# Turning sorted token rows by a transposing DMA instead of on TensorE, in a fused attention and mixture-of-experts kernel

## The chip, the cores and the metric

The kernel runs on one core of a Trainium2 chip. The metric is the device time of one execution in microseconds, from the first to the last work of the core; smaller is better. Each engine of the core (TensorE = PE, VectorE = DVE, ScalarE = ACT, GpSimd = POOL, SyncE = SP) has its own instruction stream, and they meet at semaphores. SP does no arithmetic here: it issues DMAs.

## The reference

Input are 8 x 1024 tokens of 128 channels, in float32. The layer is

```
xn  = layernorm(x)
out = x + attention(xn) + ffn(xn)

attention: off = xn @ W_off, w = softmax(xn @ W_attn) over 4 points of 8 heads
           s[token] = sum over 32 of  xn[batch, first token, idx(off)] * w
           result = broadcast(s) @ W_out + b_out

ffn(x, w1, w2, w3) = silu(x @ w1.T) * (x @ w3.T) @ w2.T       (128 -> 256 -> 128)
ffn part:  two shared experts for every token,
           + top 2 of 8 routed experts, weighted by a softmax over the 2 logits
```

## The kernel before, in words

Matmuls with float32 accuracy are made of fp16 ones: every token row x is kept as a high half and a low half (fp16 each), every weight too, and a first-layer product is three matmuls, high x high, high x low, low x high. The second layer multiplies float32 tiles.

The work goes in three stages. First (to about 85 us of the profile) x is loaded, normalised, split, turned and projected. Then (to about 257 us) the two shared experts run for 16 blocks of 512 tokens, and beside them the routing, the attention's gather (one-hot matrices that 32 transposing DMAs of line 459 turn) and the sorting: GpSimd scatters all 8192 token rows to the DRAM tensor `sorted_rows`, so that tokens with the same pair of experts stand together. A row of it has 137 words: 64 words with the 128 high halves, 64 with the 128 low halves, 8 expert weights, and the token's place in the output (`CW` = 128, `DEST` = 136).

The last stage, the one that is changed, runs the routed experts. The sorted rows are 64 tiles of 128 rows. A main job is one tile with the two experts of its first row: 24 first-layer matmuls, 8 second-layer matmuls. Where another pair begins inside a tile, 27 extra experts are done in 14 extra jobs, which load their tiles a second time. The list is `JOBS`, 78 jobs: main tiles 0 to 7, the 14 extra jobs, main tiles 8 to 63.

The first layer wants the tokens with the channels on the partitions, so each tile must be turned. Two main tiles make a step (32 steps). "Turn" n is the n-th entry of `TURN_ORDER` (46 entries: 4 main steps, 14 extras, 28 main steps). For each turn, before:

- SP loads it in the loop of lines 481 to 495: `rows<-sorted_rows` (line 485) for a main step, up to two `proj<-sorted_rows` (line 478) for an extra job. It runs up to `AHEAD` = 8 turns ahead, and waits for `d_turn`, the count of turns done on PE (line 483). The same loop issues the 16 writes of the attention's part of the output, `out_dram<-base` (line 471, `write_block`), at turns listed in `WRITE_AT`; the last two come right after the load of turn 26.
- PE turns it (`r_turn`, line 700: four transposes of 128 x 128 against the identity, to PSUM), counts `d_turn`.
- ACT copies the result from PSUM to a ring of four slots `xrT` in `units` (`r_xt`, line 886), counts `d_xt`.
- PE reads the ring in the first layer (`r_first`, lines 724 to 726).

PE's stream is software pipelined: iteration s does turn of job s, then the second layer of job s-4 (`r_second`, line 751), then the first layer of job s-2. After each job ACT applies silu (line 900), DVE multiplies (`r_hf`, line 1342, the tile `hbuf`) and, after the second layer, adds the result with its weight to `yt` in two steps (`y_first`, `y_second`, lines 1386 and 1404, for extras 1393 and 1409). Iterations 0 to 21 of DVE also add the attention's part (line 1415). The expert weights come from the same loaded rows (`side_products`, line 1354). The matrix `sides`, which these need, is made once by two PE matmuls (`spread_sides`, line 684), as part of turn 0, and an ACT copy (line 889).

GpSimd sends each finished tile to the output by an accumulating scatter (`r_send`, line 951). It starts when all 16 blocks of line 471 have landed (`out_done`) and the last extra job (job 21) is added, and then follows `d_y`, one scatter a main tile.

Of the kernel before, what the change touches and what calls it, by code (L numbers as in the profile page):

```python
# [44 lines left out]
NE = E + NSH  # L45
# [3 lines left out]
RING = 4  # L49
# [13 lines left out]
CW, DEST = 128, 136  # L63
UNROLL = 8
# [149 lines left out]
def layer_kernel(nc, x, wall, wproj, bproj, w_out, b_out, const, out, sorted_rows, y_rows):  # L214
    with ExitStack() as ctx:
# [87 lines left out]
        xr = rows[:].rearrange("p (r k) w -> p r k w", k=2)  # L303
        xrT = units[:, 4:6, :].bitcast(F16).rearrange("p i c -> p (i c)").rearrange("p (r k s c) -> p r k s c", r=RING, k=2, s=2)
# [14 lines left out]
        xr16 = xr.bitcast(F16)  # L319
        xr32 = xr.bitcast(F32)  # L320
# [93 lines left out]
        sorted_steps = sorted_rows.rearrange("(s k p) w -> s p k w", k=2, p=P)  # L414
        sorted_tiles = sorted_rows.rearrange("(t p) w -> t p w", p=P)
        out_rows = out.rearrange("b s c -> (b s) c")

        def rows_landed(eng, step):

            n = TURN_ORDER.index(step)  # L420
            before = sum(1 if s < MAIN_STEPS else min(2, EXTRAS - 2 * (s - MAIN_STEPS)) for s in TURN_ORDER[n % AHEAD:n + 1:AHEAD])
            eng.wait_ge(d_in[n % AHEAD], 16 * before)

        def rows16_of(job, k):

            return xr16[:, job.step, k] if job.main else xe16[:, 2 * job.i + k]
# [5 lines left out]
        def _(sp):  # L432
# [48 lines left out]
            for n, step in enumerate(TURN_ORDER):  # L481
                if n >= AHEAD:
                    sp.wait_ge(d_turn, n + 1 - AHEAD)
                if step < MAIN_STEPS:
                    sp.dma_start(xr[:, step], sorted_steps[step]).then_inc(d_in[n % AHEAD], 16)
                else:
                    if step == MAIN_STEPS:
                        sp.wait_ge(hot_ready, BATCH)
                        sp.wait_ge(aw_ready, 2 * BATCH)
                        sp.wait_ge(extras_ready, 1)  # L490
                    for a in range(2 * (step - MAIN_STEPS) + 1, min(2 * (step - MAIN_STEPS) + 2, EXTRAS) + 1):
                        load_extra(a, d_in[n % AHEAD])
                for i in range(NB):
                    if n == WRITE_AT[i]:
                        write_block(i)
# [6 lines left out]
        def _(pe):  # L502
# [185 lines left out]
            def r_turn(g, r):  # L688

                job = JOBS[UNROLL * g + r]  # L690
                if not job.turns:
                    return
                rows_landed(pe, job.step)
                if job.turn == 0:
                    pe.wait_ge(w_split, NE)
                if job.turn >= 2:
                    pe.wait_ge(d_xt, job.turn - 1)
                for k in range(2 if job.main else job.experts):
                    for s in range(2):
                        mm = pe.transpose(pT16[:, job.turn % 2, k, s, :], rows16_of(job, k)[:, s * P:(s + 1) * P], c["ident"][:])  # L700
                mm.then_inc(d_turn, 1)
                if job.turn == 0:
                    spread_sides()

            def r_first(g, r):
# [3 lines left out]
                pe.wait_ge(d_xt, job.turn + 1)  # L709
# [53 lines left out]
        def _(act):  # L763
# [110 lines left out]

            def r_xt(g, r):

                job = JOBS[UNROLL * g + r]
                if not job.turns:
                    return
                act.wait_ge(d_turn, job.turn + 1)  # L880
                if job.turn == 0:
                    act.wait_ge(v_done, APAIRS)
                if job.turn >= RING:
                    act.wait_ge(d_l1, LAST_OF_TURN[job.turn - RING] + 1)
                n = 2 if job.main else job.experts
                nc.scalar.copy(xrT[:, job.turn % RING, 0:n], pT16[:, job.turn % 2, 0:n]).then_inc(d_xt, 1)  # L886
                if job.turn == 0:
                    act.wait_ge(sides_done, 1)
                    nc.scalar.copy(sides.rearrange("p t k e -> p (t k e)"), pY[:].rearrange("p b c -> p (b c)")).then_inc(sides_ready, 1)
# [17 lines left out]
        def _(pool):  # L907
# [36 lines left out]
            def r_send(job):  # L944

                t = job.t
                pool.wait_ge(d_y, max(job.place, LAST_EXTRA) + 1)
                if t >= OUT_SEMS:
                    pool.wait_ge(d_out[t % OUT_SEMS], 16 * (t // OUT_SEMS))
                pool.sem_inc(pool_go, 1)  # L950
                pool.indirect_dma_start(out_rows, bass.IndirectOffsetOnAxis(ap=xr[:, job.step, t % 2, DEST:DEST + 1].bitcast(U32), axis=0),  # L951
                                        yt[:, t], None, bounds_check=TOK - 1, oob_is_err=False,
                                        compute_op=ALU.add).then_inc(d_out[t % OUT_SEMS], 16)
# [10 lines left out]
        def _(dve):  # L964
# [380 lines left out]
            def side_products(g, r):  # L1345

                job = JOBS[UNROLL * g + r]
                if job.main and job.turns:
# [5 lines left out]
                    v.tensor_tensor(side_scr[:, job.step % 2], xr32[:, job.step, :, CW:CW + E].unsqueeze(2).broadcast_to([P, 2, 2, E]),  # L1354
# [108 lines left out]
```

## Time and profile before

| | |
|---|---|
| median of 3 runs | 462.47 us (460.53 to 462.51) |
| the profiled execution's own time | 464.75 us |
| its span in the profile | 462.9 us |
| PE busy, of the span | 392.8 us (85%) |
| DVE busy | 344.3 us (74%) |
| ACT busy | 173.4 us (37%) |
| POOL busy | 198.5 us (43%) |
| mean clock granted to PE | 0.946 of full |

The profile is of one execution. Busy shares are means over three stages with different limits, so the last stage (from about 258 us to the end) must be read by itself. Matmul durations overlap (each is shown from its start to its modelled end), so what one costs is the distance between starts, which the chain of waits shows.

### The profile page before, as it was taken

The numbers are of one execution on the slowest core, as the hardware profiler recorded it, in microseconds if no ns is written. First come the engines' busy times: TensorE is split into PE (matmuls) and PEld (weight loads), VectorE is DVE, ScalarE is ACT, GpSimd is POOL, SyncE is SP. The second block draws the span as 40 slices with busy tenths as digits, with TensorE's granted clock in tenths as the row PEclk, the third lists the DMA queues.
The fourth block names the chain that finished last, engine by engine and source line by source line (L and its number), as shares of the span: only waits on it lengthen the run. The fifth ranks groups of instructions, "written<-read, shape, count | busy, mean of one in ns | idle before, by whom it ended". The sixth has DMA issues, their size and how long they took to land.

```text
span 462.9 us, 12949 instructions
## 1 busy us (share of the span) xinstructions
PE 392.8 (85%) x4485; PEld 331.9 (72%) x4485; DVE 344.3 (74%) x1093; ACT 173.4 (37%) x321; POOL 198.5 (43%) x169
## 2 busy tenths in 40 slices
PE   0555876797899999998959899999999999999990
PEld 0445733464566776666638699999999999999990
DVE  5976898989847689999999878875554555555561
ACT  3797754147212222221202334443333334333330
POOL 0432402054856544344360000002888876666664
PEclk9965897899999999999988999999999999999995
DMA  8700000010245557777626154443555554432332
GB/s 298 187 2 1 1 1 1 0 33 23 65 145 96 101 120 146 145 144 130 128 30 140 44 151 151 126 130 79 72 62 62 63 69 56 66 31 26 31 31 23
DMA packets 68791, 37.14 MB, mean 80 GB/s; under 512 B 39425, under 2 KB 62337, under 8 KB 68737
## 3 DMA queue, kind: packets, MB, share of 16 engines
q1 hardware_dynamic: 57040, 27.62, 25.3%
q0 software_dynamic: 11264, 8.69, 14.1%
q8 instruction: 34, 0.56, 0.5%
q14 instruction: 21, 0.16, 0.1%
q10 hardware_dynamic: 432, 0.11, 0.1%
HBM read 15.13 MB, written 12.88 MB: 61 GB/s over the span
## 4 chain that ended last, share of the span: by engine, by line
PE 52%; DVE 31%; issue 6%; ACT 6%; POOL 1%; DMA 1%; DVEq 1%; POOLq 0%; ACTq 0%
PE pY L751 16%; PE pAB L724 8%; PE pAB L726 8%; PE pAB L725 7%; DVE hbuf L1073 5%; ACT units L789 4%; DVE small L1257 4%; DVE aw L1241 3%; PE pY L591 3%; DVE hot L1228 3%; PE pAB L576 2%; PE pAB L578 2%; PE pAB L577 2%; PE pV L700 2%; DVE attn_all L1267 2%
## 5 line engine op out<-in xcount | busy, mean ns | idle before, releaser
L951 POOL DMA_INDIRECT out_dram<-xT,rows x64 | 99.0, 1547 | 105.6 <-DVE xT L1393 68.2
L724 PE MATMUL pAB<-units,wsp 128*128 128x128 f16 x620 | 108.4, 219 | 0.6 <-issue 0.2
L726 PE MATMUL pAB<-units,wsp 128*128 128x128 f16 x620 | 108.4, 219 | 0.0
L725 PE MATMUL pAB<-units,wsp 128*128 128x128 f16 x620 | 108.4, 219 | 0.0
L936 POOL DMA_INDIRECT sorted_rows<-rows,slot x64 | 70.0, 1094 | 82.4 <-DVE hbuf L1073 55.5
L1342 DVE SCALAR_TENSOR_TENSOR hbuf<-pAB,units 128x512 f32<-128x512 f32 x78 | 53.7, 688 | 67.8 <-PE pAB L726 52.2
L853 ACT ACTIVATE units<-pAB 128x512 f32<-128x512 f32 x64 | 38.0, 596 | 137.0 <-PE pAB L578 113.7
L751 PE MATMUL pY<-wsp,hbuf 128*128 (+1 forms) x620 | 86.9, 282 | 1.4 <-DVE xT L1404 0.7
L900 ACT ACTIVATE units<-pAB 128x512 f32<-128x512 f32 x78 | 46.4, 594 | 102.8 <-PE pAB L726 102.8
L751 PEld LDWEIGHTS pY<-wsp,hbuf 128*128 128x128 f32 x620 | 75.6, 192 | 2.3 <-issue 0.9
L576 PE MATMUL pAB<-xT,wsp 128*128 (+1 forms) x128 | 50.5, 394 | 26.4 <-DVE hbuf L1073 26.1
L591 PE MATMUL pY<-wsp,hbuf 128*128 128x128 f32 x512 | 71.5, 284 | 0.0
L591 PEld LDWEIGHTS pY<-wsp,hbuf 128*128 128x128 f32 x512 | 67.0, 196 | 4.7 <-issue 0.3
L1073 DVE SCALAR_TENSOR_TENSOR hbuf<-pAB,units 128x512 f32<-128x512 f32 x64 | 49.9, 781 | 16.7 <-ACT units L853 8.2
L724 PEld LDWEIGHTS pAB<-units,wsp 128*128 (+1 forms) x620 | 60.8, 98 | 2.0 <-issue 1.5
L725 PEld LDWEIGHTS pAB<-units,wsp 128*128 (+1 forms) x620 | 60.7, 98 | 0.9
L726 PEld LDWEIGHTS pAB<-units,wsp 128*128 (+1 forms) x620 | 60.6, 98 | 0.1
L577 PE MATMUL pAB<-xT,wsp 128*128 (+1 forms) x128 | 50.2, 392 | 0.0
L578 PE MATMUL pAB<-xT,wsp 128*128 (+1 forms) x128 | 50.0, 391 | 0.0
L576 PEld LDWEIGHTS pAB<-xT,wsp 128*128 128x128 f16 x128 | 12.8, 100 | 39.7 <-DVE hbuf L1073 22.0
L886 ACT COPY units<-pV 128x512 f16<-128x512 f16 (+1 forms) x46 | 26.7, 581 | 19.5 <-PE pV L700 19.4
L914 POOL TENSOR_TENSOR rows<-units,rows 128x512 f32 (+1 forms) x16 | 17.9, 1120 | 35.3 <-DVE rows L1050 35.3
(150 smaller groups left out, 538.3 us busy)
## 6 DMA issues: line engine op xcount, KB each, us to landing
rows<-sorted_rows SPq DMA_DIRECT2D x32, 137.0 KB
base<-in_x SPq DMA_DIRECT2D x8, 512.0 KB, 7.5
out_dram<-base SPq DMA_DIRECT2D x16, 256.0 KB, 2.5
wraw<-in_wall SPq DMA_DIRECT2D x10, 256.0 KB
proj<-sorted_rows SPq DMA_DIRECT2D x27, 68.5 KB
wsp<-in_wall SPq DMA_DIRECT2D x10, 128.0 KB
sorted_rows<-rows,slot POOLq DMA_INDIRECT x64
out_dram<-xT,rows POOLq DMA_INDIRECT x64
```

What stands on the lines that cost most here:

```text
L576: pe.matmul(bank[:, u % 2, :], whi[:, x, w], xi(0), start=True, stop=False)
L577: pe.matmul(bank[:, u % 2, :], whi[:, x, w], xi(1), start=False, stop=False)
L578: mm = pe.matmul(bank[:, u % 2, :], wlo[:, x, w], xi(0), start=False, stop=True)
L591: mm = pe.matmul(o, hbuf[:, u % 4, t], second[:, h, x, :], start=False, stop=(u % 4 == 3), skip_group_check=True)
L724: pe.matmul(o, hi, x(0), start=True, stop=False)
L725: pe.matmul(o, hi, x(1), start=False, stop=False)
L726: mm = pe.matmul(o, lo, x(0), start=False, stop=True)
L751: mm = pe.matmul(o, hbuf[:, q % 4, c0:c0 + P], w, start=(h == 0), stop=(h == 1))
L936: pool.indirect_dma_start(sorted_rows, bass.IndirectOffsetOnAxis(ap=slot[:, t:t + 1].bitcast(U32), axis=0), rows[:, t, :], None, bounds_ch ...
L951: pool.indirect_dma_start(out_rows, bass.IndirectOffsetOnAxis(ap=xr[:, job.step, t % 2, DEST:DEST + 1].bitcast(U32), axis=0), yt[:, t], No ...
L1073: v.scalar_tensor_tensor(hbuf[:, u % 4, :], pB[:, u % 2, :], 1 / (XS * WS), silu[:, u % 2, :], ALU.mult, ALU.mult).then_inc(hf_done, 1)
L1342: v.scalar_tensor_tensor(hbuf[:, q % 4, 0:job.cols], pAB[:, 2 * (q % 2) + 1, 0:job.cols], 1 / (XS * WS), silu[:, q % 2, 0:job.cols], ALU.m ...
```

## The change

For main steps the transposing is taken off PE and ACT. SP now issues two DMAs a step: one of the 9 last words of each row (`meta`, weights and destination), and one transposing DMA that reads the 256 fp16 halves of 256 rows and writes them turned to a place of their own for every step (`xrT` is now the first 64 x 128 words of `rows`, `meta` the last 64 x 9). There is no ring for them, and `r_first` waits for the landing itself. Extra jobs stay as they were, with the ring renamed `xeT`. SP's look-ahead now waits for `d_l1`, the first layer of the last job of the turn eight before, in place of `d_turn`. `spread_sides` stands at the head of the first layer of job 0, and the copy of `sides` ahead of ACT's loop.

```diff
-        xr = rows[:].rearrange("p (r k) w -> p r k w", k=2)
-        xrT = units[:, 4:6, :].bitcast(F16).rearrange("p i c -> p (i c)").rearrange("p (r k s c) -> p r k s c", r=RING, k=2, s=2)
+        row_words = rows[:].rearrange("p t w -> p (t w)")
+        xr_flat = row_words[:, 0:TILES * CW].bitcast(F16)
+        xrT = xr_flat.rearrange("p (r s k c) -> p r s k c", r=MAIN_STEPS, s=2, k=2)
+        meta = row_words[:, TILES * CW:TILES * ROWW].rearrange("p (t m) -> p t m", m=META)
+        xeT = units[:, 4:6, :].bitcast(F16).rearrange("p i c -> p (i c)").rearrange("p (r k s c) -> p r k s c", r=RING, k=2, s=2)
...
+        sorted_halves = sorted_rows.bitcast(F16).rearrange("(s q) w -> s q w", q=2 * P)
...
             for n, step in enumerate(TURN_ORDER):
                 if n >= AHEAD:
-                    sp.wait_ge(d_turn, n + 1 - AHEAD)
+                    sp.wait_ge(d_l1, LAST_OF_TURN[n - AHEAD] + 1)
                 if step < MAIN_STEPS:
-                    sp.dma_start(xr[:, step], sorted_steps[step]).then_inc(d_in[n % AHEAD], 16)
+                    sp.dma_start(meta[:, 2 * step:2 * step + 2], sorted_steps[step][:, :, CW:ROWW]).then_inc(d_in[n % AHEAD], 16)
+                    sp.dma_start(xrT[:, step].rearrange("p s k c -> p s (k c)"), sorted_halves[step][:, 0:2 * P],
+                                 transpose=True).then_inc(d_in[n % AHEAD], 16)
...
             def r_turn(g, r):
 
                 job = JOBS[UNROLL * g + r]
-                if not job.turns:
+                if job.main:
                     return
                 rows_landed(pe, job.step)
-                if job.turn == 0:
-                    pe.wait_ge(w_split, NE)
-                if job.turn >= 2:
-                    pe.wait_ge(d_xt, job.turn - 1)
-                for k in range(2 if job.main else job.experts):
+                if job.i >= 2:
+                    pe.wait_ge(d_xt, job.i - 1)
+                for k in range(job.experts):
...
                 mm.then_inc(d_turn, 1)
-                if job.turn == 0:
-                    spread_sides()
 
             def r_first(g, r):
...
-                pe.wait_ge(d_xt, job.turn + 1)
+                if q == 0:
+                    pe.wait_ge(w_split, NE)
+                    spread_sides()
+                if not job.main:
+                    pe.wait_ge(d_xt, job.i + 1)
+                elif job.turns:
+                    rows_landed(pe, job.step)
...
-                        x = lambda s: xrT[:, job.turn % RING, job.t % 2 if job.main else k, s, :]
+                        x = lambda s: xrT[:, job.step, s, job.t % 2, :] if job.main else xeT[:, job.i % RING, k, s, :]
...
+            act.wait_ge(sides_done, 1)
+            nc.scalar.copy(sides.rearrange("p t k e -> p (t k e)"), pY[:].rearrange("p b c -> p (b c)")).then_inc(sides_ready, 1)
+
             def r_xt(g, r):
 
                 job = JOBS[UNROLL * g + r]
-                if not job.turns:
+                if job.main:
                     return
...
-                n = 2 if job.main else job.experts
-                nc.scalar.copy(xrT[:, job.turn % RING, 0:n], pT16[:, job.turn % 2, 0:n]).then_inc(d_xt, 1)
-                if job.turn == 0:
-                    act.wait_ge(sides_done, 1)
-                    nc.scalar.copy(sides.rearrange("p t k e -> p (t k e)"), pY[:].rearrange("p b c -> p (b c)")).then_inc(sides_ready, 1)
+                nc.scalar.copy(xeT[:, job.i % RING, 0:job.experts], pT16[:, job.i % 2, 0:job.experts]).then_inc(d_xt, 1)
```

Two places show how the instruction streams move. On PE, late in the last stage, where the turn of a main step stood ahead of a second layer (names are output <- inputs; the rows named ISA are register work, which sets the address of the next expert's weights). Before:

```order
L726 MATMUL pAB<-units,wsp 128x128
L672 ISA
L700 MATMUL pV<-c_ident,rows 128x128 [waits d_xt,d_in4]
L700 MATMUL pV<-c_ident,rows 128x128 x3
L751 MATMUL pY<-wsp,hbuf 128x128 [waits d_y,d_hf]
L677 ISA
```

and with the change:

```order
L730 MATMUL pAB<-rows,wsp 128x128
L674 ISA
L755 MATMUL pY<-wsp,hbuf 128x128 [waits d_y,d_hf]
L679 ISA
L755 MATMUL pY<-wsp,hbuf 128x128
L679 ISA
```

The four transposes of a main step are gone, and the landing of the rows (`d_in4`) is now waited for by the first matmul of the first layer. On SP, at the two last writes of line 471, before:

```order
L485 DMA rows<-sorted_rows 128x2x137 [waits d_turn]
L471 DMA out_dram<-base 128x512 [waits attn_added]
L485 DMA rows<-sorted_rows 128x2x137 [waits d_turn] x2
L471 DMA out_dram<-base 128x512 [waits attn_added] x2
L485 DMA rows<-sorted_rows 128x2x137 [waits d_turn] x19
```

and with the change:

```order
L485 DMA rows<-sorted_rows 128x2x9 [waits d_l1]
L486 DMA_TRANSPOSE rows<-sorted_rows 128x2x256
L471 DMA out_dram<-base 128x512 [waits attn_added]
L485 DMA rows<-sorted_rows 128x2x9 [waits d_l1]
L486 DMA_TRANSPOSE rows<-sorted_rows 128x2x256
L485 DMA rows<-sorted_rows 128x2x9 [waits d_l1]
L486 DMA_TRANSPOSE rows<-sorted_rows 128x2x256
L471 DMA out_dram<-base 128x512 [waits attn_added] x2
```

Each load is two DMAs, and the two last writes now stand behind a wait for `d_l1` instead of `d_turn`.

## Rows read from the trace of the kernel before

**Rows 1.** The page, part 1: busy time, share of the span, instructions.

```profile
PE 392.8 (85%) x4485; PEld 331.9 (72%) x4485; DVE 344.3 (74%) x1093; ACT 173.4 (37%) x321; POOL 198.5 (43%) x169
```

**Rows 2.** Windows of the last stage: length, engines' busy time, granted clock, DMA share, GB/s.

```profile
260.00:275.00 15.00, 14.44 (x183) 12.60 (x182) 11.39 (x39) 5.79 (x10) 0.00 (x0) 1.00 0.44 112
275.00:315.00 40.00, 40.00 (x572) 39.72 (x570) 32.46 (x119) 18.46 (x33) 0.00 (x0) 1.00 0.47 145
315.00:360.00 45.00, 44.31 (x624) 43.83 (x624) 25.27 (x76) 16.41 (x28) 32.54 (x21) 1.00 0.47 60
360.00:400.00 40.00, 40.00 (x570) 39.81 (x568) 22.39 (x66) 14.83 (x25) 28.53 (x19) 1.00 0.51 65
400.00:450.00 50.00, 50.00 (x708) 49.59 (x707) 28.30 (x84) 17.74 (x30) 31.74 (x21) 1.00 0.34 32
```

**Rows 3.** The chain of waits, 366 to 385 us: start, length, what.

```profile
370.67 0.95 PE pY L751 x8
372.95 0.22 PE pV L700 x4
373.18 0.95 PE pY L751 x8
375.46 0.95 PE pY L751 x8
...
377.75 0.22 PE pV L700 x4
```

**Rows 4.** PE in order of time, 256 to 260 us: start, length, instructions, idle before.

```profile
258.46 0.38 PE L700 MATMUL pV<-c_ident,rows 128*128 128x128 f16 x4 [0.56 <-issue]
259.54 0.59 PE L684 MATMUL pY<-hot,c_ones 128*128 128x512 f16 x2 [0.69 <-DVE base L1083]
259.97 0.39 PE L700 MATMUL pV<-c_ident,rows 128*128 128x128 f16 x4
```

**Rows 5.** Groups by line, whole program: busy us, mean ns, idle before.

```profile
L700 PE MATMUL pV<-c_ident,rows 128*128 128x128 f16 x128 | 12.4, 219 | 0.6 <-issue 0.6
L886 ACT COPY units<-pV 128x512 f16<-128x512 f16 (+1 forms) x46 | 26.7, 581 | 19.5 <-PE pV L700 19.4
```

**Rows 6.** SP's DMAs: line 459 (issue ns min/median/max; landing), then line 485's first four.

```profile
L459 SPq DMA_TRANSPOSE units<-hot x32: 1232/1350/1904, 144.9 to 247.6; - x32
...
DMA to landing us min/median/max: 3.2/3.8/5.8
...
248.99 2.15 SPq L485 DMA_DIRECT2D rows<-sorted_rows  x4
```

**Rows 7.** Windows with four transposing DMAs (145 to 155), with four row loads (249 to 252).

```profile
145.00:150.00 5.00, 5.00 (x33) 3.41 (x31) 5.00 (x24) 1.19 (x2) 3.31 (x4) 1.00 0.88 143
150.00:155.00 5.00, 5.00 (x34) 3.63 (x32) 4.09 (x15) 1.32 (x3) 2.51 (x3) 1.00 1.03 156
...
249.00:252.00 3.00, 3.00 (x33) 2.16 (x32) 2.96 (x12) 0.60 (x1) 0.00 (x0) 1.00 0.95 209
```

**Rows 8.** SP's last two writes (line 471), their landing, and DVE after job 23.

```profile
311.20 0.94 SPq L471 DMA_DIRECT2D out_dram<-base  x2
...
DMA to landing us min/median/max: 2.1/2.5/4.5
...
319.20 0.69 DVE L1342 SCALAR_TENSOR_TENSOR hbuf<-pAB,units 128x512 f32<-128x512 f32 x1 [0.40 <-PE pAB L726]
```

**Rows 9.** POOL in order of time: scatters 1, 29, 30 and 64 of line 951.

```profile
321.12 1.58 POOL L951 DMA_INDIRECT out_dram<-xT,rows  x1 [68.25 <-DVE xT L1393]
...
373.05 1.55 POOL L951 DMA_INDIRECT out_dram<-xT,rows  x1 [0.30 <-issue]
375.55 1.54 POOL L951 DMA_INDIRECT out_dram<-xT,rows  x1 [0.95 <-DVE xT L1404]
...
455.97 1.54 POOL L951 DMA_INDIRECT out_dram<-xT,rows  x1 [0.31 <-DMA out_dram<-xT,rows]
```

**Rows 10.** POOL's sorting scatters, 140 to 235 us, beside the transposing DMAs: ns min/median/max.

```profile
L936 POOL DMA_INDIRECT sorted_rows<-rows,slot x41: 966/971/1407, 140.0 to 231.8; - x41
```

More of the change, by code:

```diff
@@ L63 @@
 CW, DEST = 128, 136
+META = ROWW - CW
 UNROLL = 8
@@ L318, in layer_kernel @@
         rows32 = rows[:].bitcast(F32)
-        xr16 = xr.bitcast(F16)
-        xr32 = xr.bitcast(F32)
+        meta32 = meta.bitcast(F32)
         xe16 = xe.bitcast(F16)
@@ L420, in rows_landed @@
             n = TURN_ORDER.index(step)
-            before = sum(1 if s < MAIN_STEPS else min(2, EXTRAS - 2 * (s - MAIN_STEPS)) for s in TURN_ORDER[n % AHEAD:n + 1:AHEAD])
+            before = sum(2 if s < MAIN_STEPS else min(2, EXTRAS - 2 * (s - MAIN_STEPS)) for s in TURN_ORDER[n % AHEAD:n + 1:AHEAD])
             eng.wait_ge(d_in[n % AHEAD], 16 * before)
-        def rows16_of(job, k):
-            return xr16[:, job.step, k] if job.main else xe16[:, 2 * job.i + k]
         block = ctx.enter_context(nc.Block())
@@ L869, in _ @@
             straight(UNITS, UNITS + 3, both)
+            act.wait_ge(sides_done, 1)
+            nc.scalar.copy(sides.rearrange("p t k e -> p (t k e)"), pY[:].rearrange("p b c -> p (b c)")).then_inc(sides_ready, 1)
             def r_xt(g, r):
                 job = JOBS[UNROLL * g + r]
-                if not job.turns:
+                if job.main:
                     return
-                act.wait_ge(d_turn, job.turn + 1)
-                if job.turn == 0:
+                act.wait_ge(d_turn, job.i + 1)
+                if job.i == 0:
                     act.wait_ge(v_done, APAIRS)
-                if job.turn >= RING:
-                    act.wait_ge(d_l1, LAST_OF_TURN[job.turn - RING] + 1)
-                n = 2 if job.main else job.experts
-                nc.scalar.copy(xrT[:, job.turn % RING, 0:n], pT16[:, job.turn % 2, 0:n]).then_inc(d_xt, 1)
-                if job.turn == 0:
-                    act.wait_ge(sides_done, 1)
-                    nc.scalar.copy(sides.rearrange("p t k e -> p (t k e)"), pY[:].rearrange("p b c -> p (b c)")).then_inc(sides_ready, 1)
+                if job.i >= RING:
+                    act.wait_ge(d_l1, [j.place for j in JOBS if j.i == job.i - RING][0] + 1)
+                nc.scalar.copy(xeT[:, job.i % RING, 0:job.experts], pT16[:, job.i % 2, 0:job.experts]).then_inc(d_xt, 1)
             def r_silu(g, r):
@@ L950, in r_send @@
                 pool.sem_inc(pool_go, 1)
-                pool.indirect_dma_start(out_rows, bass.IndirectOffsetOnAxis(ap=xr[:, job.step, t % 2, DEST:DEST + 1].bitcast(U32), axis=0),
+                pool.indirect_dma_start(out_rows, bass.IndirectOffsetOnAxis(ap=meta[:, t, DEST - CW:DEST - CW + 1].bitcast(U32), axis=0),
                                         yt[:, t], None, bounds_check=TOK - 1, oob_is_err=False,
@@ L1353, in side_products @@
                         dve.wait_ge(share_ready, job.step - 1)
-                    v.tensor_tensor(side_scr[:, job.step % 2], xr32[:, job.step, :, CW:CW + E].unsqueeze(2).broadcast_to([P, 2, 2, E]),
+                    v.tensor_tensor(side_scr[:, job.step % 2], meta32[:, 2 * job.step:2 * job.step + 2, 0:E].unsqueeze(2).broadcast_to([P, 2, 2, E]),
                                     sides[:, 2 * job.step:2 * job.step + 2], ALU.mult).then_inc(side_parts, 1)
```

2 lines of the change are left out of this document (1 added, 1 removed).

## The prediction

> **What bounds the kernel now.** I read the page first, then the windows of the last stage, then the chain of waits there. The page gives PE as the busiest engine [rows 1], but 85% over the whole span does not say where it is the limit. The windows do: from 275 us to 450 us PE is busy in 40.00 of 40.00, 44.31 of 45.00, 40.00 of 40.00 and 50.00 of 50.00 us, at the full granted clock (1.00, 2.4 GHz), while DVE has 32.46 of 40.00 at first and then some 56% [rows 2]. The reader should see two things: no engine but PE is full, and the clock column leaves no room for a gain or a loss by the clock. The chain then shows what PE's time is made of. From one second layer to the next PE needs 2.29 us a job (373.18 to 375.46), and in front of every other job stand four transposes of line 700, 0.22 us long (372.95); two jobs take 377.75 - 372.95 = 4.80 us [rows 3]. Nothing but PE stands in that piece of the chain. So in this stage a microsecond off PE is a microsecond off the end, until another engine or a load is late.
>
> **What is removed.** The 32 main steps have 4 transposes each, 128 in all [rows 5]. The busy column there (12.4 us) overstates them, since matmuls overlap; the distance in the chain, 0.22 us for four, is what they cost [rows 3]. One of the 32 turns is free today: turn 0 runs at 258.46, while PE would wait anyway for DVE's line 1083 (the idle 0.69 before line 684 at 259.54) [rows 4]. Turn 1, at 259.97, stands between `spread_sides` and the first first layer and counts [rows 4]. That leaves 31 x 0.22 = 6.8 us. ACT loses 32 copies of 0.58 us, 18.6 us [rows 5], but it is busy for some 37% there [rows 2], so I cost this at nothing. The cover is PE: the copy is never in the chain.
>
> **What is added on SP and the DMA engines.** No transposing DMA from DRAM is in the trace; the nearest rows are the 32 that turn `hot` inside SBUF, of 256 KB each, twice the bytes of a step. Their issue takes 1.35 us (at most 1.90), and they land after 3.8 us (at most 5.8) [rows 6]. Half the size gives an issue between 0.7 and 1.90 us; I take 1.35, the row itself. The second new DMA, 256 pieces of 36 bytes, I take like the row load it replaces, 2.15 / 4 = 0.54 us an issue [rows 6]. A step is then 1.2 to 2.4 us of SP, of 4.57 us (two jobs): SP keeps up. In DMA time, four transposing DMAs of 256 KB and some sorting scatters filled (0.88 + 1.03) x 5 = 9.6 us, 2.4 each at most, so 1.2 us for half; four row loads took 0.95 x 3 = 2.9 us, 0.71 each [rows 7], and the small one takes between nothing and that. So a step costs 1.2 to 1.9 us of all DMA engines where it cost 0.71, and the share of 0.51 [rows 2] rises by 0.11 to 0.26. There is room. The Trainium skill ("Advanced Engine Details and Errata", X-Bar Transpose) says that transposing DMAs are as fast as regular ones. The rows disagree here: 1.2 us against 0.71 us for about the same bytes. By its rule the share would hardly rise, and the sum would be the same.
>
> **The start.** SP issues its first loads at 249.0 [rows 6]. The first step has landed at 249.0 + 0.54 + 1.35 + 3.8 = 254.7, at worst (1.90, 5.8) 257.2. PE asks for it at 259.8 or so, right after `spread_sides` [rows 4]. Hidden, with 2.6 us to spare at worst. The four steps occupy SP until 249.0 + 4 x 1.9 = 256.6, at worst 258.8; the extra loads behind them start at about 259.5 anyway, as they wait for DVE.
>
> **The moved look-ahead.** The wait for `d_l1` releases a load two or three jobs later than `d_turn` did. By the job list a main load is released at least 8 jobs before its first layer (turn 18), from turn 26 on 15 jobs: 18 to 34 us against a landing of 5.8 [rows 3, 6]. Extras 4 to 13 have 5 jobs or more, 11 us. Nothing there. What stands behind that wait on SP are the two last writes of line 471. They follow the load of turn 26, which now waits for the first layer of job 23. That ends just before DVE's 319.20 [rows 8], less the five turns already saved, so at 318.0. Add 0.54 + 1.35 for the load, 0.94 for the writes and 2.5 for their landing (at most 4.5) [rows 8]: POOL may start at 323.3, at worst at 325.9, where it started at 321.12. Its scatters come 1.85 us apart while it catches up ((373.05 - 321.12) / 28), and from the 30th on it waits for DVE [rows 9]. Unhindered, the 64th could start at 323.3 + 63 x 1.85 = 440, at worst 442.5. PE lets it start at 455.97 - 6.8 = 449.2. So the catching up only ends later, and the delay is hidden with 7 us to spare.
>
> **The sum.** 464.75 - 6.8 = 458.0 us for an execution like the profiled one, whose time is 2.3 us above the median of the runs. Against the median: 462.47 - 6.8 = **455.7 us**. The tail behind the last job is unchanged, and moves with PE.
>
> **The rivals.**
>
> *Loads too slow (the other side).* If the loads run one behind another at T us a step, the last of the 28 late steps is needed 8 x 2.29 + 27 x 4.57 = 142 us after the first is released, so they are hidden up to T = 142 / 28 = 5.06. Beyond that each tenth of a microsecond costs 2.8 us, and from 5.30 the kernel is slower than before. If each one waited for the landing of the one before, at the longest landing in the rows, T = 5.8 [rows 6], the end comes 28 x 0.74 - 6.8 = 13.9 us later: 476.4. For it: DRAM rows of 548 bytes are read, which no transposing DMA does today. Against it: SP issued four `hot` transposes within about 6 us though each landed after 3.8 [rows 6], so they overlap, and the four were through in under 10 us with twice the bytes [rows 7]. Chance 0.06.
>
> *Block by block.* A milder form of the same: the crossbar turns the four 128 x 128 blocks of a step in series. It would have to need over 5.06 / 4 = 1.27 us a block, against 10 / 32 = 0.3 in the rows [rows 7]. Between 1.27 and 1.33 us a block the end lies between 455.7 and 462.5. Chance 0.03. The Trainium skill ("VectorE: DVE Perf Modes", The three transpose paths) gives 1309 ns for a crossbar block and 390 ns on TensorE, and its rules for authors advise TensorE where PSUM will do. With its figure T is 5.24 us and 5.0 us of the gain are lost, an estimate of 460.7. The trace contradicts both figures: 0.3 us, and 0.055 us a transpose in PE's stream.
>
> *GpSimd becomes the bound.* Its scatters would share the DMA engines with the transposing DMAs. The sorting scatters did so: 0.97 us in the median, 1.41 at most [rows 10]. If every scatter until the last load (about 36 of them) took 0.44 us more, the 64th would start at 440 + 16 = 456 to 458.5, nothing gained or 2.5 us lost: 462.5 to 465. It decides from a mean pace of 2.0 us. Against it: the median row shows no slowing. Chance 0.06.
>
> *A second bound close behind PE.* DVE has little air in the first jobs, 11.39 of 15 us and 32.46 of 40 [rows 2], and after job 21 its waits for PE are not long (0.40 at 319.20) [rows 8]. If half of the gain stays hanging there: 459.1. Against it: the tight jobs are extras, whose turns stay, and later DVE has 44% free. Chance 0.07.
>
> That the change does not do what it says can be left out: the instruction order shows the transposes gone.
>
> **How the numbers follow.** The forecast keeps 0.78. About 0.5% (2.3 us) is what a measurement of this kernel can tell from no change; faster means below 460.2, slower above 464.8. Faster: 0.78 + 0.05 of the second bound + 0.01 block by block = 0.84. Same: 0.02 + 0.02 + 0.04 of GpSimd = 0.08. Slower: 0.06 + 0.02 of GpSimd = 0.08. The range: the three runs before lie 2 us apart, so a gain of 6.8 may be read from 453.5 on; if the small PE gaps go too, a little lower, 453.2. The upper end takes in the second bound: 459.6.
>
> **What would show it.** Right: in the chain the rows of 0.22 us between second layers are gone and every main job takes 2.29 us; PE stays full from 275 us to about 443 us; `r_first` never waits for a DMA; POOL starts 2 to 5 us later against PE's work and catches up at about 400 us instead of 375. Wrong: PE idle in front of the first layer with a DMA as releaser (loads), most of all at job 0 or late; POOL scatters of line 951 back to back, or longer than 1.55 us, until the end (GpSimd); a job distance over 2.4 us with waits for `hbuf` or `xT` (second bound).

## The result, and the profile after

The changed kernel takes 455.6 us in the median of 4 runs, the kernel before 461.63 us (4 runs, the three above and one more beside it): 6.0 us less, a ratio of 0.987, 95% interval 0.983 to 0.990. Forecast were 455.7 us and "faster by over 0.5%" with a chance of 0.84; both held. The gain measured is a little smaller than the 6.8 us of the sum. That the forecast lies within 0.1 us is luck: the median of before that it started from, 462.47, was 0.8 us above the one found with the fourth run, and this made up for a gain that was put 0.8 us too high. Two repeats on slower chips gave less, 4.9 and 4.3 us (0.989 and 0.990, see the experiments); the three intervals overlap. One of the four runs of the changed kernel took 1104 us instead of 455; the ratio leaves it out (the median of the other three is 455.44), and what became of it is told under the hardware.

The page of the changed kernel, part 1, to be read beside [rows 1]:

```profile
PE 385.1 (85%) x4357; PEld 325.4 (72%) x4357; DVE 344.7 (76%) x1093; ACT 155.0 (34%) x289; POOL 197.9 (44%) x169
```

128 instructions fewer on PE, 32 fewer on ACT, and ACT's busy time down by 18.4 us. The windows of the last stage, which answer to [rows 2] (columns as there; this execution is 3.2 us ahead when the stage begins, see below):

```profile
260.00:275.00 15.00, 14.98 (x198) 14.61 (x197) 11.88 (x40) 4.28 (x8) 0.00 (x0) 0.92 0.26 70
275.00:315.00 40.00, 39.83 (x568) 39.49 (x567) 31.93 (x117) 16.72 (x30) 0.00 (x0) 1.00 0.54 139
315.00:360.00 45.00, 44.42 (x620) 44.03 (x618) 25.95 (x78) 11.84 (x20) 32.34 (x21) 1.00 0.69 73
360.00:400.00 40.00, 40.00 (x560) 39.79 (x560) 24.27 (x72) 10.15 (x17) 33.30 (x23) 1.00 0.61 67
400.00:440.00 40.00, 39.86 (x561) 39.48 (x559) 23.43 (x68) 10.44 (x18) 27.21 (x18) 1.00 0.38 38
```

PE is full as before, at the full clock but for the first window (0.92). The DMA share is up by 0.22 and 0.10 in the two middle windows. And the chain of waits, against [rows 3]:

```profile
366.78 0.95 PE pY L755 x8
369.06 0.95 PE pY L755 x8
371.35 0.95 PE pY L755 x8
```

The rows of 0.22 us are gone; from one second layer to the next it is 2.29 us for every job.

**Where the time came from.** The profiled executions differ by 9.3 us (464.75 and 455.44), more than the medians. The rest is not the change's: 3.2 us are there before the last stage starts. They are there already when SP comes to its last four transposes of line 459 (240.40 us instead of 243.56), ahead of everything that was changed; the profiled execution of the kernel before was itself 3.1 us above its median. Three marks divide the last stage, the end of DVE's last shared sum (line 1083, now 1086) and the multiplications `hbuf` of jobs 22 and 77. In the kernel before (VectorE in order of time; start, length):

```profile
258.71 0.68 DVE L1083 SCALAR_TENSOR_TENSOR base<-pY,base 128x512 f32<-128x512 f32 x1
...
317.36 0.69 DVE L1342 SCALAR_TENSOR_TENSOR hbuf<-pAB,units 128x512 f32<-128x512 f32 x1 [1.27 <-PE pAB L726]
...
449.81 0.69 DVE L1342 SCALAR_TENSOR_TENSOR hbuf<-pAB,units 128x512 f32<-128x512 f32 x1 [0.95 <-PE pAB L726]
```

and in the changed one:

```profile
255.54 0.68 DVE L1086 SCALAR_TENSOR_TENSOR base<-pY,base 128x512 f32<-128x512 f32 x1
...
313.75 0.69 DVE L1345 SCALAR_TENSOR_TENSOR hbuf<-pAB,units 128x512 f32<-128x512 f32 x1 [1.28 <-PE pAB L730]
...
440.41 0.69 DVE L1345 SCALAR_TENSOR_TENSOR hbuf<-pAB,units 128x512 f32<-128x512 f32 x1 [0.95 <-PE pAB L730]
```

| us | before | changed | difference |
|---|---|---|---|
| end of line 1083 / 1086 to `hbuf` of job 22 | 57.97 | 57.53 | 0.4 |
| `hbuf` of job 22 to job 77 | 132.45 | 126.66 | 5.8 |
| `hbuf` of job 77 to the end of the span | 13.1 | 13.2 | -0.1 |
| last stage | 203.5 | 197.4 | 6.1 |

The last line agrees with the medians. In the 55 jobs from 22 to 77 stood 26 turns, 5.8 / 26 = 0.22 us each. Ahead of `hbuf` of job 22 stood five turns that could count, and they gave 0.4 us together instead of 1.1.

SP and POOL in the changed kernel (SP: issue ns min/median/max and landing of line 486; then SP and POOL in order of time):

```profile
L486 SPq DMA_TRANSPOSE rows<-sorted_rows x32: 1186/1187/2147, 246.4 to 403.8; - x32
...
DMA to landing us min/median/max: 2.8/3.0/3.3
...
315.98 1.69 SPq L486 DMA_TRANSPOSE rows<-sorted_rows  x1
317.71 1.05 SPq L471 DMA_DIRECT2D out_dram<-base  x2
```

```profile
321.56 1.58 POOL L954 DMA_INDIRECT out_dram<-xT,rows  x1 [72.06 <-DMA out_dram<-base]
...
401.26 1.54 POOL L954 DMA_INDIRECT out_dram<-xT,rows  x1 [0.31 <-issue]
403.37 1.55 POOL L954 DMA_INDIRECT out_dram<-xT,rows  x1 [0.56 <-issue]
...
446.57 1.54 POOL L954 DMA_INDIRECT out_dram<-xT,rows  x1 [0.31 <-DMA out_dram<-xT,rows]
```

POOL starts at the landing of the last write (the releaser is now `out_dram<-base`), 65.3 us after the stage's mark instead of 61.7, runs back to back until 403, and is in step with DVE after that. The delay is there and costs nothing.

### The profile page after: what moved, and what is told of

Read it like the earlier page. It is cut to its first block, busy times and chain, and to the rows that moved or that the text cites. A ratio compares the mean times of both kernels' runs of the same rounds, so it can differ in the third digit from the quotient of the medians.

```text
span 453.6 us, 12596 instructions
## 1 busy us (share of the span) xinstructions
PE 385.1 (85%) x4357; PEld 325.4 (72%) x4357; DVE 344.7 (76%) x1093; ACT 155.0 (34%) x289; POOL 197.9 (44%) x169
## 4 chain that ended last, share of the span: by engine, by line
PE 57%; DVE 28%; ACT 6%; issue 5%; POOL 1%; DMA 1%; DVEq 1%; POOLq 0%; ACTq 0%
PE pY L755 16%; PE pAB L728 8%; PE pAB L730 8%; PE pAB L729 8%; PE pY L593 5%; DVE hbuf L1076 4%; ACT units L793 4%; PE pAB L578 3%; PE pAB L580 3%; PE pAB L579 3%; DVE small L1260 3%; DVE aw L1244 3%; DVE hot L1231 2%; DVE attn_all L1270 2%; ACT xT L801 1%
## 5 line engine op out<-in xcount | busy, mean ns | idle before, releaser
L939 POOL DMA_INDIRECT sorted_rows<-rows,slot x64 | 69.3, 1083 | 80.1 <-DVE hbuf L1076 55.9
L728 PE MATMUL pAB<-rows,wsp 128*128 128x128 f16 x512 | 90.6, 221 | 0.4
L730 PE MATMUL pAB<-rows,wsp 128*128 128x128 f16 x512 | 90.7, 221 | 0.0
L729 PE MATMUL pAB<-rows,wsp 128*128 128x128 f16 x512 | 90.6, 221 | 0.0
L728 PEld LDWEIGHTS pAB<-rows,wsp 128*128 x512 | 50.5, 99 | 1.7 <-issue 1.5
L729 PEld LDWEIGHTS pAB<-rows,wsp 128*128 x512 | 50.5, 99 | 0.7
L730 PEld LDWEIGHTS pAB<-rows,wsp 128*128 x512 | 50.5, 99 | 0.2
L1244 DVE SCALAR_TENSOR_TENSOR aw<-proj 128x128 f32 (+1 forms) x128 | 28.7, 287 | 2.4 <-DVE attn L1260 2.2
```

What stands on the lines that cost most here:

```text
L728: pe.matmul(o, hi, x(0), start=True, stop=False)
L729: pe.matmul(o, hi, x(1), start=False, stop=False)
L730: mm = pe.matmul(o, lo, x(0), start=False, stop=True)
L939: pool.indirect_dma_start(sorted_rows, bass.IndirectOffsetOnAxis(ap=slot[:, t:t + 1].bitcast(U32), axis=0), rows[:, t, :], None, bounds_ch ...
```

## The experiments

Each is measured together with runs of the kernel before on the same chip, and chips differ by some 4 us (the kernel before takes 461.6 to 461.8 us on some, 465.3 to 465.5 on others). So ratios are compared between chips; times are compared only on one chip, or between chips on which the kernel before took the same (455.6 us is the changed kernel's where before takes 461.6 to 461.8).

**Is it PE's work that was saved?** Idle transposes at the head of the first layer:

```diff
...
+                if job.main and job.turns:
+                    for k in range(4):
+                        pe.transpose(pAB16[:, 2 * (q % 2), k * P:(k + 1) * P], c["ident"][:], c["ident"][:])
                 for bank, col, done in ((2 * (q % 2), W1, d_a), (2 * (q % 2) + 1, W3, d_l1)):
```

> The changed kernel, with four idle 128x128 fp16 transposes of the identity (their output is overwritten) in front of the first layer of every step's first main job: PE's old work without ACT's copies and without the waits. Theory (PE is the bound, four transposes cost 0.22 us on its stream): 32 x 0.22 = 7.0 us more than the changed kernel, about 462.5 us, level with the kernel before; the chain shows 0.22 us per step again. Rival (the gain came from ACT's copies or from the waits on the ring, not from PE's work): no more than 1 us over the changed kernel, 455.5 to 456.6.

466.79 us, beside 460.58 for the changed kernel and 465.49 for the one before on the same chip: 6.2 us more than the changed kernel, 1.002 of before (1.001 to 1.004). Its chain has the rows of 0.22 us again, once in 4.8 us:

```profile
370.43 0.22 PE pAB L721 x4
375.22 0.22 PE pAB L721 x4
```

PE's 0.22 us a step is the gain; the rival is out. The 7.0 us expected were too many in the same way as the prediction's sum: from `hbuf` of job 22 to that of job 77 the profile has 5.75 us more than the changed kernel's on this chip, and before that only 0.7, for five turns.

**ACT's copies.** The old work put back beside the new loads. Shown is ACT's part; on PE the idle transposes stand at the old places and wait for the copy of two turns before. Not put back are the first layer's wait for its own copy and the copy's wait for its place in the ring.

```diff
...
+                if job.main:
+                    idle = wraw[:].bitcast(F16).rearrange("p r (u k s c) -> p (r u) k s c", k=2, s=2, c=P)
+                    nc.scalar.copy(idle[:, job.turn % RING, 0:2], pT16[:, job.turn % 2, 0:2]).then_inc(d_xt, 1)
+                    return
```

> The changed kernel with the whole old work put back beside the new loads: idle transposes of the identity to PSUM at the old places, ACT's 32 copies of them to a spare tile, and the waits between them. Theory (ACT's copies are hidden): the same time as with the idle transposes alone, within 1 us, 461.5 to 462.6. Rival (ACT's copies or the two-buffer waits have a price): over 1 us more than with the transposes alone.

464.93 us, 0.999 of before (0.998 to 1.001), and its last stage takes 203.5 us by the marks above, like the one before the change. Loads by transposing DMA, the moved look-ahead and the moved waits by themselves cost or give nothing that can be measured. The rival fell: the copies add no time, the kernel is even 1.9 us faster than with the transposes alone, more than the 1 us allowed. The two differ in the place of the transposes too (here at the old place, where turn 0 lies in PE's gap, there always in front of the first layer). In the two profiles only 1.0 us of the difference lies in the last stage (203.5 against 204.5), and 1.8 us ahead of it, where the kernels are alike; what makes either was not separated.

**How long may a load take?** The look-ahead is cut for the last 18 loads, to 2 turns and to 1:

```diff
-                    sp.wait_ge(d_l1, LAST_OF_TURN[n - AHEAD] + 1)
+                    sp.wait_ge(d_l1, LAST_OF_TURN[n - (2 if n >= 28 else AHEAD)] + 1)
```

> The changed kernel with SP's look-ahead cut from 8 turns to 2 for the last 18 loads (turn 28 on): a load is released when the first layer of the turn two before is done, which is 2 jobs and a second layer (5.5 us) ahead of its use. Theory (a load takes 0.4 us for the small DMA's issue and lands 3.0 us after the transposing one's issue, so some 3.6 us, and loads overlap): hidden, the changed kernel's time within 1 us, 0.988 of before. Rival (loads from DRAM come one behind another at 5.8 us a step): each of the 18 is 1.2 us late or more, over 20 us added, ratio over 1.03.

456.1 us, 0.987 of before (0.984 to 0.991), against 455.6: hidden, with a quarter of the look-ahead.

> The same with a look-ahead of one turn: the load is released 0.95 us before its use (one second layer), so its whole duration but that shows as a wait of PE, 18 times. Theory: 3.6 - 0.95 = 2.7 us each, 48 us in all, 1.09 of before; PE's waits name the DMA. It measures the duration on which the prediction's threshold of 5.06 us a step rested. Rival (block by block, 1.31 us a block, 5.2 us a step and the latency on top): over 4.3 us each, 77 us or more.

523.9 us in the median of two runs, 1.134 of before (1.125 to 1.143): 68 us more than the changed kernel, between the 48 of the theory and the 77 of the rival. The waits separate the parts. Who waited for whom in this kernel, 325 to 520 us (us in total, times, longest), and one such load and wait in order of time (SP, then PE):

```profile
PE pAB L728 <- DMA rows<-sorted_rows: 52.0, 18, 4.0
...
393.44 0.37 SPq L485 DMA_DIRECT2D rows<-sorted_rows  x1
393.85 1.86 SPq L486 DMA_TRANSPOSE rows<-sorted_rows  x1
...
397.21 0.23 PE L728 MATMUL pAB<-rows,wsp 128*128 128x128 f16 x1 [2.86 <-DMA rows<-sorted_rows]
```

The waits are 2.9 us in the mean (2.7 expected), and the load shown takes 3.8 us from the small DMA's issue to the first matmul. That is near the theory's 3.6. The rest is not waiting for loads. In this profile 197.1 us lie between `hbuf` of job 22 and of job 77, 70.5 more than in the changed kernel's, and 52.0 of them are the waits. PE waits for little else there (1.8 us), but it runs at a lower granted clock after the waits:

```profile
360.00:400.00 40.00, 24.91 (x286) 24.02 (x287) 12.70 (x37) 5.38 (x9) 21.60 (x14) 0.90 0.38 42
...
325.00:520.00 195.00, 136.15 (x1636) 130.98 (x1632) 72.34 (x209) 30.48 (x51) 97.45 (x63) 0.92 0.33 36
```

It was 1.00 in the changed kernel. An estimate from the mean of 0.92: (1 - 0.92) x 195 = 15.6 us of full clock are missing, most of the 18.5 us that the waits leave. The theory had left that out.

**How much air has POOL?** The two last writes, four turns later:

```diff
+WRITE_AT[14] = WRITE_AT[15] = 30
 LAST_EXTRA = max(job.place for job in JOBS if not job.main)
```

> The changed kernel with the last two writes of the attention's part (line 471) behind the load of turn 30 instead of 26, eight jobs or 18.3 us later. POOL's output scatters wait for them. Theory (POOL has 7 us of slack and from then on 1.85 us a scatter sets the end): start at 321.6 + 18.3 = 339.9, the 64th scatter at 339.9 + 63 x 1.85 = 456.5 instead of 446.6, so 10 us more than the changed kernel, 1.010 of before; scatters back to back to the end. Rival (scatters can go faster when a backlog is there, or the end does not hang on them): within 2 us of the changed kernel, 0.988 to 0.992 of before.

465.72 us, 1.008 of before (1.005 to 1.010), 10 us above the changed kernel's 455.6. The first and the last scatter (POOL in order of time):

```profile
341.00 1.58 POOL L955 DMA_INDIRECT out_dram<-xT,rows  x1 [90.78 <-DMA out_dram<-base]
...
457.77 1.54 POOL L955 DMA_INDIRECT out_dram<-xT,rows  x1 [0.30 <-issue]
```

(457.77 - 341.00) / 63 = 1.853 us a scatter, to the end. Counted from the end of the last shared sum, POOL starts 17.8 us later than in the changed kernel and the stage is 9.5 us longer (206.9 against 197.4), so the slack was 8.3 us. The look-ahead's wait is not free of danger: put more than that in front of these two writes and GpSimd sets the end.

**Do the transposing DMAs slow the scatters?** Each one from turn 28 on issued twice, the second time to a place that nobody reads:

```diff
...
+                    if n >= 28:
+                        sp.dma_start(spare[:, n - 28].rearrange("p (s q) -> p s q", s=2), sorted_halves[step][:, 0:2 * P],
+                                     transpose=True).then_inc(spare_in, 16)
```

> The changed kernel with every transposing DMA from turn 28 on issued twice, the second time into a place that nobody reads. Theory (there is room on SP and the DMA engines, and POOL's scatters are not slowed): SP 2.75 us of 4.57 a step, DMA share in 325 to 400 us up by about 0.2, scatters still 1.55 us long and 1.85 us apart, time of the changed kernel within 1 us, 0.988 of before. Rival (GpSimd's scatters suffer from transposing DMAs): scatters longer than 1.55 us or further apart while loads run, time up by several us.

455.28 us, 0.985 of before (0.982 to 0.989). The window and POOL's group (320 to 453 us):

```profile
360.00:400.00 40.00, 40.00 (x561) 39.79 (x561) 24.25 (x72) 10.15 (x17) 33.30 (x23) 1.00 0.90 97
...
L962 POOL DMA_INDIRECT out_dram<-xT,rows x64 | 99.1, 1548 | 99.5 <-DMA out_dram<-base 71.9 <-issue 18.2 <-DVE xT L1415 6.9
```

The DMA share goes from 0.61 to 0.90 and the scatters stay at 1.548 us each. The second DMA of a step costs 0.29 x 4.57 = 1.3 us of all DMA engines, near the 1.2 that the prediction took. Two such DMAs go through SP's queue in each step of 4.57 us and nothing is late, so one takes no more than 2.3 us of the queue.

**The gap in front of the first job.** In the changed kernel turn 0 no longer stands in the gap before line 686. PE in order of time, and the window after it:

```profile
256.37 0.59 PE L686 MATMUL pY<-hot,c_ones 128*128 128x512 f16 x2 [1.64 <-DVE base L1086]
...
259.00:262.00 3.00, 3.00 (x28) 2.53 (x28) 2.21 (x8) 0.60 (x2) 0.00 (x0) 0.50 0.39 93
```

The same window has a clock of 1.00 in the kernel before (columns as in [rows 2]). Filling the gap:

```diff
...
                 if job.main:
+                    if job.turn == 0:
+                        for k in range(24):
+                            pe.transpose(pF16[:, 0, k // 2 % 2, k % 2, :], c["ident"][:], c["ident"][:])
                     return
```

> The changed kernel with 24 idle transposes (1.3 us of PE work) in the gap of 1.64 us that PE has before the matmuls of line 686. In the changed kernel's profile the granted clock is 0.50 from 259 to 262 us, right after that gap; before the change turn 0 stood in it and the clock was 1.00. Theory (the gap that turn 0 used to fill brings the clock down): clock 1.00 in that stretch, the second hbuf multiplication comes 5.5 us after the end of the last shared sum instead of 6.5, the time is about 1 us less than the changed kernel, 454.6. Rival (the clock falls for another reason, or the first jobs are limited by address work and DVE): same time within 0.3 us, whatever the clock.

460.7 us, beside 460.58 for the changed kernel on the same chip: nothing. And the changed kernel's own profile on that chip has the same gap, 1.64 us, with a full clock behind it:

```profile
261.65 0.59 PE L686 MATMUL pY<-hot,c_ones 128*128 128x512 f16 x2 [1.64 <-DVE base L1086]
...
262.00:264.00 2.00, 1.62 (x15) 0.88 (x14) 1.35 (x6) 1.05 (x2) 0.00 (x0) 1.00 0.32 70
```

So the fall comes in some executions only, and costs little: `hbuf` of job 1 comes 6.48 us after the mark with it, 5.84 without, but by job 7 the two are 0.13 us apart (20.98 and 20.85). The theory of a microsecond to be had here fell by this comparison. The filler does not test it, because it did not do what was meant: both jobs of the first step have turn 0, so 48 transposes ran and not 24, longer than the gap,

```profile
259.47 2.84 PE L697 MATMUL pV<-c_ident 128*128 128x128 f16 x48 [0.42 <-issue]
```

with the clock at 1.00 throughout, and `hbuf` of job 7 came 0.7 us later than without it (21.57). What a filler of the right length would do is not known. All profiles together: in 11 kernels and repeats with this gap of 1.64 us the clock fell after it in six and stayed full in five; in the three with PE work in the gap (the kernel before, the old work put back, the filler) it never fell. That fits the gap as a condition of the fall, but three are few.

**The changed kernel again**, twice:

> The changed kernel once more, in more rounds beside the kernel before: 455.6 us, 6 us less than before (ratio 0.987). One of its first four runs took 1104 us. If that belongs to the kernel (a transposing DMA that stalls now and then), it comes back in some of these runs and in other kernels with these loads; if it was an accident of the machine, in none.

460.58 us beside 465.49, 0.989 of before (0.987 to 0.991), 5 runs.

> The changed kernel beside the two variants on the same chip: 0.987 to 0.988 of before. None of its runs is expected near 1104 us, if that one was an accident of the machine.

461.03 us beside 465.32, 0.990 of before (0.988 to 0.993), 6 runs.

These are gains of 4.9 and 4.3 us, where 6 were expected. By the marks above the last stage takes 198.0 and 198.4 us in these two profiles against 197.4 in the first one, and nearly all of the difference lies between jobs 22 and 77 (127.5 and 127.7 us against 126.7). The kernel before was not profiled on these chips, so what makes the gain smaller there stays open.

**Can the extras go the same way?** Two variants. In one each of the 27 extra tiles has a small and a transposing DMA; in the other the small DMAs are gathered (four, for tiles 8 to 63), and the extras' weights are read from them:

```diff
-                    sp.dma_start(xe[:, a - 1], sorted_tiles[bass.ds(at, 1)].rearrange("o p w -> p (o w)")).then_inc(landed, 16)
+                    sp.dma_start(xeT[:, a - 1], sorted_tile_halves[bass.ds(at, 1)][:, :, 0:2 * P].rearrange("o p w -> p (o w)"),
+                                 transpose=True).then_inc(landed, 16)
...
```

> The changed kernel with the extras by transposing DMA in the plain way: for each of the 27 extra tiles a small DMA of the last 9 words and a transposing one. Theory (SP becomes late): about 1.7 us of SP a tile, 46 us for 27, and the writes between them; the last two writes come some 8 us later than in the changed kernel, POOL starts at about 330 us and its 64 scatters at 1.85 us set the end: as slow as the changed kernel or up to 4 us slower, 0.987 to 0.996 of before, scatters back to back to the end. Rival (SP has room): 2 to 3 us less than the changed kernel, like the variant with fewer small DMAs.

480.71 us, 1.032 of before (1.029 to 1.035): 20 us slower than the changed kernel, where the theory had at most 4. The side was right, the size not. The theory took 1.7 us of SP a tile; from one tile's small DMA to the next it is 2.2 us (261.52 to 263.74), without the writes between them. POOL starts at 356.6, not at 330, and its 64 scatters run back to back to 473.4.

> The changed kernel with the 14 extra jobs served by transposing DMAs too (one per extra tile, no turn on TensorE, no ACT copy), and with the 9 last words of tiles 8 to 63 loaded by four DMAs at the start instead of one per step, from which the extras' weights are then read by tile number. It gives SP about the number of DMAs it has in the kernel before. Theory (PE is the bound in the extras too): 14 x 0.22 = 3.1 us less than the changed kernel, less what DVE (2.2 us of work a job there, against 2.29) takes back; 2 to 3 us, about 0.981 of before. Rival (DVE becomes the bound as soon as the turns are gone): under 1 us less, the distance between hbuf multiplications of extras stays near 2.5 us.

463.05 us, 0.995 of before (0.993 to 0.997): 2 us slower than the changed kernel. Both expectations fell. SP in order of time and by line (the second variant), and PE's waits for DMAs in it and in the first (250 to 330 us):

```profile
262.65 19.82 SPq L477 DMA_TRANSPOSE proj<-sorted_rows  x12
...
L477 SPq DMA_TRANSPOSE proj<-sorted_rows x27: 1167/1176/1882, 262.6 to 311.8; - x27
...
PE pAB L718 <- DMA proj<-sorted_rows: 3.2, 3, 1.5
```

```profile
PE pAB L716 <- DMA proj<-sorted_rows: 10.9, 6, 3.4
```

A transposing DMA of one tile (64 KB) holds SP for 1.18 us, as long as one of two tiles (1.19). An extra job needs two. With the register loads that is 1.4 to 1.65 us a tile, about 3 us a job, where PE leaves 2.3 to 2.5. SP falls behind; PE waits 3.2 us (10.9 in the first variant, where its clock also drops to 0.66 from 305 to 320 us). The two last writes are issued at 330.5, and POOL starts at 336.9 and then sets the end.

The last experiment takes the writes off SP:

```diff
+            def r_write(g, r):
+
+                q = UNROLL * g + r
+                for i in range(NB):
+                    if q == -(-TPB * (i + 1) // ADDS) + 1:
+                        act.wait_ge(attn_added, i + 1)
+                        act.dma_start(out_blk[i], base_blk[:, i, :]).then_inc(out_done, 16)
+
+            pipeline(act, NJOB, UNROLL, NJOB // UNROLL, [(0, r_write), (2, r_silu)])
...
```

> The variant with all jobs by transposing DMA and few small DMAs, with the 16 writes of the attention's part (line 471) moved from SP's queue to ACT's. In that variant a transposing DMA held SP 1.19 us whether it moved 64 or 128 KB, so the 27 extra ones and the writes took SP more than the 2.29 us a job that PE leaves it. Theory (SP's issue time was the bound there): the 15 tiles from 282 us on take SP 1.4 us each and end 10 us ahead of their use, no wait of PE for a DMA, an extra job takes 2.3 us instead of 2.57, POOL starts earlier than in the changed kernel and follows DVE before the end: 2 to 3 us less than the changed kernel, 0.982 to 0.985 of before. Rival (DVE, with 2.2 us of work in these jobs, is the bound behind PE): extra jobs stay at 2.45 us or more, level with the changed kernel, 0.988 to 0.990.

454.74 us beside 461.64 for the kernel before: 0.985 (0.983 to 0.988). No wait of PE for a DMA is left, and POOL follows DVE. But an extra job still takes 2.405 us. VectorE in order of time (the multiplications `hbuf`, and the end of the second addition), and the second layers in the chain:

```profile
287.08 0.69 DVE L1323 SCALAR_TENSOR_TENSOR hbuf<-pAB,units 128x512 f32<-128x512 f32 x1 [0.27 <-PE pAB L712]
...
288.88 0.34 DVE L1393 SCALAR_TENSOR_TENSOR xT<-pY,hot,xT 128x128 f32 x1
289.49 0.69 DVE L1323 SCALAR_TENSOR_TENSOR hbuf<-pAB,units 128x512 f32<-128x512 f32 x1 [0.27 <-PE pAB L712]
...
291.89 0.69 DVE L1323 SCALAR_TENSOR_TENSOR hbuf<-pAB,units 128x512 f32<-128x512 f32 x1 [0.27 <-PE pAB L712]
```

```profile
287.02 1.06 PE pY L737 x8
289.43 1.06 PE pY L737 x8
```

The second layer (289.43) starts 0.21 us after the second addition ends (289.22), and 2.46 us later (291.89) comes the second `hbuf` after the one of 287.08. With the 2.35 us from `hbuf` (287.08) to the second layer that makes a ring of 4.81 us for two jobs. DVE and PE wait in turn for each other through the two halves of `pY`. That ring stands close behind PE: 2.405 us a job, against 2.51 with turns and 2.29 without. It is the reading of one profile; more halves of `pY` were not tried. As a version, this kernel is ahead of the kernel before by 1.5%, but its interval overlaps the changed kernel's (0.983 to 0.990), so that it beats that one is not shown.

## Why the prediction was right, point by point

- **PE is the bound of the last stage, 0.22 us a turn.** Right: 5.8 us for the 26 turns between `hbuf` of jobs 22 and 77, and 6.2 us given back when the idle transposes were put in.
- **31 turns count.** Too many. The turns 1 to 3 and the two at jobs 22 and 24 gave 0.4 us instead of 1.1. By `hbuf` of job 7 three turns gave 0.2 us of 0.66 (21.19 us after the mark before, 20.98 now), and the fall of the clock takes 0.13 of what is missing. The turn at job 22 gave its 0.22 (2.51 us from `hbuf` of job 19 to that of job 20, now 2.29). The turn at job 24 gave nothing: between `hbuf` of jobs 21 and 22 it is 2.52 us before and after. It stood behind the short last extra job (one expert), and in the changed kernel PE waits at this place for DVE's second addition (PE in order of time; the second layer of job 20):

```profile
311.23 1.13 PE L755 MATMUL pY<-wsp,hbuf 128*128 128x128 f32 x8 [0.17 <-DVE xT L1412]
```

  The term should have been 26 x 0.22 and the early ones between nothing and full: 5.7 to 6.8. It measured 6.0, and only 4.9 and 4.3 in the repeats on slower chips, below that range; why is open.
- **ACT's 18.6 us cost nothing.** Right: putting them back added nothing.
- **SP and the DMA engines.** The issue was taken as 1.35 us from the nearest row and is 1.19; the landing as 3.8, and is 3.0 (2.8 to 3.3), with 3.8 from the issue of the small DMA to the first matmul. The price for the DMA engines, 1.2 us for a transposing DMA, measured 1.3, and the DMA share rose by 0.22 and 0.10 where 0.11 to 0.26 was forecast. That the rows price it higher than a plain load of the same bytes (0.71) stands. Not foreseen: the issue time hardly depends on the size (1.18, 1.19 and 1.35 us for 64, 128 and 256 KB). It did not matter here.
- **The start.** Right: nothing waits for the first load. What the text did not see is that turn 0, costed at nothing, had kept PE busy in its gap; in some executions the clock now falls to 0.50 after it. It costs 0.1 to 0.2 us by job 7. The clock column did leave room for a loss, if a small one.
- **The moved look-ahead and POOL.** Right in mechanism, and near in size. Predicted were a start at 323.3 in the time of the profile before and the end of the catching up at 400. Measured are 321.56 and 403, with 3.2 us to be added for the earlier start of the stage: 324.7 and 406. The slack, 7 us at worst by the prediction and 9 by its middle values, measured 8.3: 17.8 us of delay cost 9.5.
- **Loads too slow, block by block.** Both ruled out: a look-ahead of two turns hides the load. The threshold of 5.06 us a step was a sound way to ask, and the load is far below it: even with every late load issued twice nothing was late.
- **GpSimd becomes the bound.** Ruled out as a matter of contention (scatters unchanged at a DMA share of 0.90), but real as a matter of order: it appears as soon as the writes are over 8 us later, and it decided the end of both plain variants of the extras.
- **A second bound close behind PE.** Did not take half the gain, but it exists, at 2.405 us in the jobs that also add the attention's part, and the one turn at job 24 was lost to it.

## What to carry to other kernels

When the engine that fills a stage gives work to the DMA queues, price three things apart: the issuing engine's time for each DMA (here 1.2 us for a transposing one, of 64 or of 128 KB), the DMA engines' time, and the time from release to landing against the look-ahead. Here the first was the scarce one: two tiles in one DMA fit behind PE; one tile in each did not, until another engine issued the writes. And ask what else stands in the issuing queue behind a wait that is moved; two ordinary writes there held back GpSimd's whole output, and their slack was the real margin of the change.

## What the runs showed of the hardware that was not expected

- A transposing DMA costs its issuer nearly the same for any size seen here: 1.18 us (64 KB), 1.19 us (128 KB), 1.35 us (256 KB, inside SBUF). The time of the DMA engines grew with the bytes instead: 1.3 us for 128 KB, and at most 2.4 us for 256 KB [rows 7].
- Waits of PE cost more than their length. 18 waits of 2.9 us cost 68 us, not 52; the mean granted clock is 0.92 from 325 to 520 us, a mix of the two levels, 1.2 and 2.4 GHz.
- After an idle time of 1.64 us at the same place, the clock fell to 1.2 GHz for some 3 us in two of three profiles of the changed kernel, and in six of the 11 profiles that have this gap. The length of a gap alone does not tell it.
- One run of 1104 us among the first four of the changed kernel. In 75 later runs of kernels with these loads (11 of them of the changed kernel itself) none came back; the slowest, 527 us, was the one with a look-ahead of one turn. Its mean granted clock is on record as 1.00, where every other run has 0.92 to 0.96; it left no profile. What it was stays open; nothing shows that it belongs to the transposing DMAs.
